# Involution: the first running row maximum of a slot taken at tick 9 instead of tick 7

## The reference

```python
sub2 = x1[:, :, None] - unfold_patches(x2)            # 49 differences per pixel
...
y = conv1x1(relu(bn_eval(feat)), cw1)
y = relu(bn_eval(y))
wgt = softmax(conv1x1(y, cw2, cb2), axis=2)           # over the 49 taps
...
for i in range(7):
    for j in range(7):
        out = out + patch(x3p, i, j) * wgt[:, :, 7 * i + j]
```

## Time and profile before

| what | us |
|---|---|
| median of 3 runs (3545.55 to 3552.47) | 3547.08 |
| the profiled execution | 3520.45 |
| its span, first to last instruction | 3518.6 |
| TensorE matmul busy (x42638) | 3007.2 (85%) |
| VectorE busy (x2173) | 2525.7 (72%) |
| ScalarE busy (x3387) | 1982.6 (56%) |
| GpSimd busy (x1235) | 2166.9 (62%) |
| L689 products, busy / mean of one | 1053.7 / 3.789 |
| granted TensorE clock, mean | 0.952 |

### The profile page before, as it was taken

How to read it: one execution, slowest core, us unless ns; L and a number is a source line. 1 busy time by engine, 2 the same in 40 slices (tenths; PEclk the granted TensorE clock), 3 DMA queues, 4 the chain that set the end, 5 groups by cost and what they waited for, 6 DMA issues and landing times. The chain is left out here.

```text
span 3518.6 us, 102494 instructions
## 1 busy us (share of the span) xinstructions
PE 3007.2 (85%) x42638; PEld 1502.5 (43%) x42638; DVE 2525.7 (72%) x2173; ACT 1982.6 (56%) x3387; POOL 2166.9 (62%) x1235
## 2 busy tenths in 40 slices
PE   4987878887878877875799999999999989789997
PEld 1233434333334433432453355235434533367675
DVE  6379999999999999997864676377647657464322
ACT  1575656665656665652458755865686567534221
POOL 3378989898988888985563177117704751334433
PEclk9999999989999999999799999999999999999998
DMA  6531111211111221111212111121111111435544
GB/s 228 158 124 54 59 53 36 65 60 56 58 53 36 65 59 55 56 26 41 66 29 62 56 39 49 39 64 29 44 45 51 30 50 50 138 114 176 158 146 147
DMA packets 190699, 257.34 MB, mean 73 GB/s; under 512 B 88974, under 2 KB 151674, under 8 KB 188216
## 3 DMA queue, kind: packets, MB, share of 16 engines
q1 hardware_dynamic: 178348, 218.25, 20.5%
q0 software_dynamic: 11520, 32.55, 3.0%
q10 hardware_dynamic: 396, 0.05, 0.0%
HBM read 152.23 MB, written 79.27 MB: 66 GB/s over the span
## 5 line engine op out<-in xcount | busy, mean ns | idle before, releaser
L846 PE MATMUL ps<-late,ident 32*32 32x504 f32 x21952 | 1068.7, 640 | 248.3 <-issue 175.0
L689 DVE TENSOR_TENSOR late<-ps,late 128x3584 f32<-128x3584 f32 x280 | 1053.7, 3789 | 84.1 <-PE ps L846 75.7
L846 PEld LDWEIGHTS ps<-late,ident 32*32 32x32 f32 x21952 | 459.2, 107 | 528.0 <-issue 464.1
L319 POOL TENSOR_TENSOR late<-ex,late 128x1792 f32<-128x1792 f32 x140 | 528.6, 3775 | 40.3 <-issue 17.9
L1582 POOL TENSOR_TENSOR pool<-share 128x768 f32<-128x768 f32 (+1 forms) x200 | 349.0, 1752 | 176.7 <-ACT share L1778 130.0
L1824 ACT ACTIVATE phq<-ps 128x896 f32<-128x896 f32 x448 | 391.7, 920 | 71.4 <-PE ps L2176 67.3
L287 POOL TENSOR_TENSOR y<-xa 128x1568 f32<-128x1568 f32 x98 | 330.6, 3381 | 146.7 <-PE ps L822 145.8
L298 POOL TENSOR_TENSOR ex<-lg,mx 128x1568 f32<-128x1568 f32 x98 | 345.9, 3547 | 12.7 <-DVE mx L670 12.7
L519 ACT ACTIVATE ps<-ex 128x448 f32<-128x448 f32 x280 | 149.6, 534 | 299.0 <-DVE late L689 298.9
L2176 PE MATMUL ps<-qst,sel 96*128 96x448 bf16 x1120 | 295.0, 356 | 14.1 <-ACT phq L1824 8.4
L1927 DVE TENSOR_TENSOR pool<-ps,share 128x1280 f32<-128x1280 f32 (+1 forms) x200 | 295.4, 1480 | 4.2 <-ACT ps L1784 2.8
(11 more groups left out here) (280 smaller groups left out, 5093.1 us busy)
## 6 DMA issues: line engine op xcount, KB each, us to landing
late<-planes SPq DMA_DIRECT2D x14, 2480.0 KB, 9.0
pf<-pf_dram SPq DMA_DIRECT2D x392, 55.1 KB
planes<-ex SPq DMA_DIRECT2D x7, 1984.0 KB, 9.2
conv_dram<-late SPq DMA_DIRECT2D x56, 224.0 KB, 4.9
t<-in_x SPq DMA_DIRECT2D x28, 448.0 KB, 4.0
xt<-conv_dram SPq DMA_DIRECT2D x28, 448.0 KB, 6.8
t_dram<-tout SPq DMA_DIRECT2D x28, 448.0 KB, 2.9
pool<-t_dram SPq DMA_DIRECT2D x24, 512.0 KB, 4.4
```

Source lines behind the costliest of these rows:

```text
L319: pool.tensor_tensor(o[:, :, 0:SHARE], w.unsqueeze(2).broadcast_to([P, RW, SHARE, W]), xw, ALU.mult).then_inc(own_ready, 1)
L689: v.tensor_tensor(o, w, xw, ALU.mult).then_inc(prod_ready, 1)
L846: mm = pe.matmul(ps[32 * h:32 * h + 32, 4 + r, 0:DENC], diag(ident, r), x[32 * r:32 * r + 32, h].rearrange("p s w -> p (s w)"), start=begi ...
```

## The change

The list of ticks for the row maxima changes from 5, 7, 9, 11, 13, 15, 17 to 9, 9, 9, 11, 13, 15, 17. Since three entries are now equal, the loop that looks a tick up in the list becomes one over all entries. `rowmax(0)` is empty, so what happens is that `rowmax(1)` stands ahead of pair 9 instead of ahead of pair 7, directly followed by `rowmax(2)`. FOLD_AT and all other ticks stay.

```diff
-MAX_AT = [CH_AT[2 * i + 1] + 3 for i in range(K7)]
+MAX_AT = [CH_AT[2 * max(i, 2) + 1] + 3 for i in range(K7)]
...
                 for u in range(NPAIR_D):
-                    if a and u in MAX_AT:
-                        rowmax(MAX_AT.index(u))
+                    for i in range(K7):
+                        if a and u == MAX_AT[i]:
+                            rowmax(i)
```

## The result

The changed kernel takes 3512.14 us (median of 6 runs, 3501.94 to 3520.25), the kernel before 3546.32 (6 runs). The ratio is 0.9901, with a 95% interval from 0.9884 to 0.9918: 34 to 35 us or 1.0% faster, where 3507 had been forecast. Run again beside others it gave 0.9903 [0.9885, 0.9921]. One of the six executions of a later kernel, the one with maximum 4 at tick 12, took 7961.48 us and is left out of its ratio.

A forecast was written before the change was run, and what follows sets the result against it. VectorE was taken as the bound, its first row maxima held 60.6 us by GpSimd over 13 slots. Nine slots gaining 4.5 us each gave 40 us: 3547 - 40 = 3507 us, range 3479 to 3549.

The forecast's parts named there:

- the start: Slot's beginning up to pair 6; the forecast case gave no change there, a rival had gain lost there.
- slots near 101 us: Sign to look for in the changed trace: slot period near 101 us, against 106.2 before.
- The stretch: From start of pair 6 to end of maximum 3: forecast 28.6 us instead of 31.9, 3.3 us a slot gained.
- the remark on either order: Whether maximum 2 or z of row 5 goes first, maximum 3 ends at 671.6, 28.6 us from pair 6.
- The late part: End of maximum 3 to next slot: between 42.6 and 45.6 us, depending on maximum 4; 3.0 us between both ends.
- the forecast case: Whole kernel 22 to 60 us faster, middle 40 us from nine slots at 4.5 us; chance 0.57.
- The rival of the gain given back at the start: Half-clock at each slot's start leaves 0.8 us gain a slot, 10 us in all, median 3537; chance 0.16.
- The number of slots: Of 13 slots, nine gain 4.5 us each; four with short first maxima already gain nothing.
- The four: Slots with first maxima of 2.76 to 4.68 us, said to come late against GpSimd; given no further gain.
- the nine: Slots with long first maxima, held 7.8 us each; forecast to gain 4.5 us each, 40 us together.
- TensorE as the bound: Rival: half clock in ticks 9 to 12 behind the pair of maxima, 21 us slower, median 3568; chance 0.10.
- who was queued first: Slot 4's first maximum cost 8.56 us, not about 2: profile start order doesn't tell queue order.

## Why the prediction was right

The sign, the mechanism and, within 5 to 6 us, the size came as forecast: 34 to 35 us measured, 40 forecast. The terms of the sum came less well than their total: the start was not nothing, and slots near 101 us did not come (104.2 and 103.9).

*The stretch.* By steps, slot 4 of after beside what was worked out from slot 4 of before, counted from pair 6. z of row 5: 14.4 measured, 14.25 forecast. First maximum: asked at 12.8 (12.5), 1.78 (1.78). Second: 4.73 (4.9), z ahead of it by 0.19 (0.1). Maximum 3: asked at 26.9 (26.7), 1.97 (1.9). End: 28.9 (28.6); over the 13 slots 28.7 and 28.6 in the two profiles. In slot 8 of the first profile maximum 2 came ahead of z, 1.79, and maximum 3 took 4.91: stretch 28.84, as the remark on either order said. Holding GpSimd back by hand showed the same in all slots.

*The late part.* It lay between the ends given, 44.0 to 44.3 where 42.6 and 45.6 had been, by a form that neither slot had: maxima 4, 5 and 6 mostly ask 2.8 us into an own product and take 2.6.

*The start.* Here is the term that was mis-sized. I gave it nothing in the forecast case, it costs 0.7 us a slot on average, 9 us a kernel. Of the 9 slot 0 alone has 3.8 us in the first pair of profiles and 1.4 in the second; in the others it is 0.4 to 0.6 a slot. The rival of the gain given back at the start is this, in part: it would have left 0.8 us of gain a slot, and took 0.7 from some 3. The half-clock time at the start of slots grew from 72 us to 89 and 99. The granted clock in three stretches of after, at the start of slot 4, behind its two maxima, and at the start of slot 5:

```profile
618.80:625.60 6.80, 4.85 (x84) 2.53 (x95) 6.32 (x3) 3.02 (x2) 6.80 (x4) 0.50 0.80 332
663.20:670.00 6.80, 4.30 (x75) 2.18 (x80) 6.80 (x3) 1.79 (x3) 6.44 (x4) 0.50 0.01 2
721.20:731.40 10.20, 7.50 (x120) 2.70 (x120) 7.89 (x3) 3.86 (x3) 10.20 (x5) 0.50 0.53 223
```

In before seven of 13 slots had 3.4 us of half clock there, in after three and one. Why the clock falls longer is not settled. With z of row 5 held back the start is 30.0, and with maximum 2 at tick 10, where slots are shorter still, it is 30.5 and 30.6, so it is not tied to the shorter slot as such.

*The number of slots.* Nine with the gain, four without, was right in kind: slots 5 and 9 went from 105.3 and 105.4 to 105.3 and 103.8, slot 3 from 102.4 to 103.8, slot 0 from 108.4 to 112.0. The four lost 3.3 us together; the nine gained 29.5, 3.3 each where 4.5 had been forecast. Of that the stretch gave 2.6 (it had been 31.3 on average in the nine, 31.9 in slot 4), the late part 1.5, as the middle of its two ends had it, and the start took 0.8. The reason given for the four, that their first maxima come late against GpSimd, holds for slots 3, 5 and 9; that of slot 0 asked 0.50 us into the shift. Over all 13 slots the stretch gave 23 us in the first pair of profiles and 27 in the second (13 x 1.8 and 2.1), the late part 12 and 16, and the start took 9 each time: 26 and 34 in sum.

*TensorE as the bound* didn't come. The stretch of 6.8 us at half clock in ticks 9 and 10 is there (663.20 above), as long as the one before, and costs what was said: waits ahead of pairs 11 to 16 of 0 to 1.1 us a slot in the first profile.

The Trainium skill, page "SBUF — State Buffer", section "Who interferes with whom", has the exclusion right. The trace agrees: in all these runs a held maximum ends 1.65 us behind the end of the GpSimd instruction that holds it. The same section says that issue order decides who blocks, and this the trace does not bear out. The maximum of 646.79 had started when z of row 4 was not yet released (648.45), and z went first all the same. The prediction put it down to who was queued first; nothing here shows that.

## What to carry to other kernels

Look for instructions whose median is far above their minimum at the same shape, and lay the other engine's timeline beside them: the holder shows in which ends coincide. Put such an instruction where the other engine has a hole that the data dependences force; moved elsewhere, the hold of maximum 4 went to maximum 5 here. One wait on the other engine, so that its next instruction stays behind, was worth as much as the move. Once the worst hold is gone ask again which engine sets the period, and try moving load too: one tap from GpSimd to VectorE gave 33 us, about as much as the change.

## What the runs showed of the hardware that I had not expected

- A VectorE instruction with two SBUF operands stood behind two GpSimd instructions that both started later than it by the profile (8.56 us for 1.78 of work), the second of which was released 1.7 us after it had started; and behind one when that second one had to wait for it (5.52).
- Behind an own product the copy (L320) mostly let the maximum in and was stretched from 0.37 to 1.95 us; three maxima of 9.1 us, in the kernel with maximum 4 at tick 12, stood behind two own products and both copies. Between a shift and z the maximum got in where z was released 0.17 us or less before the shift's end, and twice where it was released 1.2 and 1.4 us before.
- TensorE's half-clock stretches in the middle of the slots, 61 and 72 us a kernel before, were gone with the maxima at ticks 9, 10 and 11, and pairs 11 to 16 waited for TensorE 0.2 us a slot at most there. Why is open.
- The stages behind the slots took 1870 to 1875 us on one chip and 1890 to 1897 on another, in twelve profiles of eleven kernels; the kernel before itself is 19 to 26 us faster on the first of them (medians 3524.9 against 3544.1 and 3550.8). The two profiles of the kernel before differ there by 18 us (1871 and 1890) while their slots sum to the same within 5.
